# Attention sums of each edge visit: added to the table in memory by GpSimd, in place of TensorE's carry products

## What is computed

```
h = relu(layernorm(x));  y = layernorm(h) * g + b;  q, k, v = split(y @ Wqkv + bqkv)   # 8 heads of 32
scores = sum_d q[src] * k[dst] * SCALE                 # one per edge and head
e      = exp(scores - max over the edges of dst)
agg    = segment_sum(v[src] * e / segment_sum(e, dst)[dst], dst)
x1     = h + agg
x      = x + x1 + feedforward(layernorm(x1))           # gelu(y @ W_in + b_in) @ W_out + b_out
# second layer: h1 = relu(layernorm(x)); messages h1 @ W[relation], summed by dst, gelu, layernorm, added to x
```

## Time and profile before

| | us |
|---|---|
| median of 3 runs | 1527.08 |
| lowest and highest | 1525.3, 1531.56 |
| the profiled execution's own time | 1523.96 |
| its span in the trace | 1522.1 |
| TensorE busy in the span | 1138.3 (75%) |
| VectorE busy | 898.6 (59%) |
| GpSimd busy | 918.3 (60%) |
| ScalarE busy | 448.1 (29%) |

### The profile page before, as it was taken

One profiled execution on the slowest core, in us unless ns is written; L12 is line 12 of the kernel. 1 busy time (PEld: TensorE's weight loads), 2 busy tenths in 40 slices (PEclk: granted clock), 3 DMA queues, 4 the chain that ended last, 5 costly groups with the idle time before them and its releaser, 6 DMA issues.

```text
span 1522.1 us, 18355 instructions
## 1 busy us (share of the span) xinstructions
PE 1138.3 (75%) x5319; PEld 846.0 (56%) x5319; DVE 898.6 (59%) x2826; ACT 448.1 (29%) x1150; POOL 918.3 (60%) x983
## 2 busy tenths in 40 slices
PE   5784879999999999999999993554645555554543
PEld 2442667777787777777777652333534334443432
DVE  5762678878887887887888630133425443442425
ACT  4652224454454444445445330000000000000000
POOL 3855666666666666666666004666666666766651
PEclk9997899999999999999999996767767876776766
DMA  7768776777877777777676212333433343343431
GB/s 243 215 188 264 214 223 210 248 238 231 272 228 239 250 237 237 229 245 220 228 252 223 78 58 72 105 110 113 123 114 112 113 116 115 115 121 108 119 95 56
DMA packets 142977, 265.55 MB, mean 174 GB/s; under 512 B 41594, under 2 KB 89828, under 8 KB 139930
## 3 DMA queue, kind: packets, MB, share of 16 engines
q0 software_dynamic: 52480, 160.68, 35.3%
q1 hardware_dynamic: 89434, 102.48, 20.7%
q10 hardware_dynamic: 960, 1.18, 0.2%
HBM read 199.25 MB, written 65.01 MB: 174 GB/s over the span
## 4 chain that ended last, share of the span: by engine, by line
DVE 31%; issue 20%; another core or an unknown queue 18%; PE 18%; ACT 5%; DMA 0%; DVEq 0%; POOL 0%; POOLq 0%; ACTq 0%
DVE arena L1807 5%; DVE arena L1812 5%; PE ps L1539 5%; DVE arena L1742 4%; PE ps L1506 3%; PE ps L1679 3%; DVE arena L1860 2%; PE ps L1565 2%; PE ps L1495 2%; DVE arena L689 2%; ACT arena L1314 1%; ACT L1298 1%; DVE arena L692 1%; DVE arena L671 1%
## 5 line engine op out<-in xcount | busy, mean ns | idle before, releaser
L1222 POOL DMA_INDIRECT arena<-qv_tab,srcs x392 | 383.3, 978 | 229.4 <-PE ps L1506 127.4
L1265 POOL DMA_INDIRECT arena<-h_all,typs x392 | 376.1, 959 | 236.2 <-issue 112.9
L1679 PE MATMUL ps<-arena 128*128 128x256 f32 x784 | 248.1, 477 | 92.2 <-DMA arena<-h_all,typs 47.5
L1679 PEld LDWEIGHTS ps<-arena 128*128 128x128 f32 x784 | 184.5, 243 | 150.5 <-issue 52.1
L1506 PE MATMUL ps<-arena 128*128 128x264 f32 x784 | 213.7, 401 | 35.3 <-DVE arena L1742 24.4
L1565 PE MATMUL ps<-wrel,arena 128*128 128x512 f32 x400 | 188.0, 595 | 2.3 <-ACT arena L1330 2.3
L1506 PEld LDWEIGHTS ps<-arena 128*128 128x128 f32 x784 | 139.3, 193 | 73.8 <-DVE arena L1742 32.0
L1742 DVE TENSOR_TENSOR arena<-arena 128x512 f32<-128x512 f32 x196 | 143.8, 734 | 40.7 <-ACT arena L1298 33.4
L1495 PE MATMUL ps<-arena 128*128 128x264 bf16 x1032 | 143.4, 280 | 12.4 <-DMA arena<-k_tab 12.2
L1495 PEld LDWEIGHTS ps<-arena 128*128 128x128 bf16 x1032 | 125.6, 145 | 46.6 <-issue 37.2
L1807 DVE TENSOR_TENSOR arena<-arena,ps 128x512 f32<-128x512 f32 x172 | 117.4, 683 | 49.1 <-remote 24.0
(11 more groups left out here) (166 smaller groups left out, 1488.1 us busy)
## 6 DMA issues: line engine op xcount, KB each, us to landing
h_all<-arena SPq DMA_DIRECT2D x23, 1024.0 KB
arena<-dst SPq DMA_DIRECT2D x49, 256.0 KB
rel<-arena SPq DMA_DIRECT2D x77, 128.0 KB
arena<-k_tab SPq DMA_DIRECT2D x49, 198.0 KB
att<-arena SPq DMA_DIRECT2D x52, 132.0 KB, 5.4
qv_tab<-arena SPq DMA_DIRECT2D x25, 256.0 KB, 3.0
arena<-qv_tab,srcs POOLq DMA_INDIRECT x392
arena<-h_all,typs POOLq DMA_INDIRECT x392
```

Of the source, the lines that this page charges most:

```text
L1222: pool.indirect_dma_start(out=rowbuf[:, u * T + t, 0:2 * D], out_offset=None, in_=qv_tab, in_offset=bass.IndirectOffsetOnAxis(ap=srcs[:, v ...
L1265: pool.indirect_dma_start(out=rows1[:, u * T + t, :], out_offset=None, in_=h_all[0:N * R, :], in_offset=bass.IndirectOffsetOnAxis(ap=typs[ ...
L1679: last = nc.tensor.matmul(ps[:, 6 + u, 0:D], ind1[:, u, t, :], rows1[:, u * T + t, :], start=(t == 0), stop=(v == 0 and t == T - 1))
```

## The change

In the fused stage `carry`, its matrix `car`, the semaphores `car_ready` and `win_done` and SP's `store` go. TensorE's sum of a visit ends with its own last tile, and ScalarE's `take` waits for that. `osum` now holds the sums of that visit alone, and GpSimd adds them to the 128 rows of `att` by a DMA that reads the rows in memory and adds (`accum_op`). It is put between tiles 1 and 2 of GpSimd's gathers three visits later; the last three come after all gathers. Each waits until the one before has landed, as before.

```diff
-            car = cut([2, WIN])
@@ SP
-                def store(v):
-                    w = window(v)
-                    sp.wait_ge(osum_ready, v + 1)
-                    if v >= 1:
-                        sp.wait_ge(att_out, 16 * v)
-                    sp.dma_start(att[bass.ds(w, WIN), :], osum[:, v % 2, :]).then_inc(att_out, 16)
...
-                    if v >= 1:
-                        store(v - 1)
...
-                store(LASTV)
@@ GpSimd, in gather(v)
+                        if t == 1 and v >= 3:
+                            add_window(v - 3)
...
+                def add_window(v):
+                    w = pool.value_load(wof[0:1, v + 1:v + 2], min_val=0, max_val=NWIN * WIN)
+                    pool.wait_ge(osum_ready, v + 1)
+                    if v >= 1:
+                        pool.wait_ge(att_out, 16 * v)
+                    pool.dma_start(att[bass.ds(w, WIN), :], osum[:, v % 2, :], accum_op=ALU.add).then_inc(att_out, 16)
...
                 for v in range(G):
                     gather(v)
+                for v in range(G - 3, G):
+                    add_window(v)
@@ ScalarE, in take(v)
-                    act.wait_ge(win_done, v + 1)
+                    act.wait_ge(agg_done, PAIRS * (v + 1))
@@ TensorE
-                                                start=(t == 0), stop=(v == 0 and t == T - 1))
+                                                start=(t == 0), stop=(t == T - 1))
...
-                def carry(v):
-
-                    if v == 0:
-                        pe.wait_ge(agg_done, PAIRS)
-                        pe.sem_inc(win_done, 1)
-                        return
-                    pe.wait_ge(osum_ready, v)
-                    pe.wait_ge(car_ready, v)
-                    nc.tensor.matmul(ps[:, AGG, 0:AW], car[:, v % 2, :], osum[:, 1 - v % 2, :], start=False, stop=True).then_inc(win_done, 1)
...
-                        carry(v)
...
-                    carry(v)
@@ VectorE
-                        if j == 0 and v >= 1:
-                            nc.vector.tensor_scalar(car[:, u, :], iotaj[:, :], wcar[:, v:v + 1], None,
-                                                    ALU.is_equal).then_inc(car_ready, 1)
```

More of the change, by code:

```diff
@@ L721, in program @@
             row_in = [sem(f"rows_in{j}") for j in range(2 * PAIRS)]
-            indT_ready, car_ready = sem("indT_ready"), sem("car_ready")
+            indT_ready = sem("indT_ready")
             turn_ready, ind_ready = sem("turn_ready"), sem("ind_ready")
             exp_done, w_ready, agg_done = sem("exp_done"), sem("weighted_ready"), sem("summed")
-            win_done, osum_ready, att_out = sem("window_done"), sem("osum_ready"), sem("att_out")
+            osum_ready, att_out = sem("osum_ready"), sem("att_out")
             zeros = sem("zeros_ready")
```

## The result

| | before | changed |
|---|---|---|
| median, us | 1526.76 (4 runs) | 1557.6 (4 runs) |
| lowest and highest | 1525.3, 1531.56 | 1554.14, 1560.63 |
| ratio, 95% interval | | 1.0196, 1.0164 to 1.0227 |
| span of the profiled run | 1522.1 | 1552.4 |

The forecast, 1517.4 us with a range of 1508 to 1538, was wrong: the time lies above the range. The kernel before itself has two levels, 1525 to 1534 us in some sets of runs and 1433 to 1438 us in others (two sets, one at each level, ran on the chip of the same number), and the changed kernel is slower at the first level and faster at the second. I call them **the 1530 level** and **the 1436 level**; ratios are always between runs of one set.

What follows compares the result with a forecast made beforehand. Each pair of visits was taken as bound in turn by VectorE and TensorE. Terms -9.9 - 1.5 - 1.3 + 0 + 1.5 + 1.5 = -9.7 us took the median 1527.08 to 1517.4 us, range 1508 to 1538.

Steps and rivals of the forecast that it cites:

- Added: GpSimd's part: GpSimd, each visit: a register load and a DMA issue, 1.85 us, fit into some 2.1 us left idle; cost 0.
- (d): GpSimd becomes the bound if an adding store's issue takes 1 us more than a gather's: 37 us, 1554 us; chance 0.07.
- Removed: the carries: TensorE, fused stage: 48 carry products go, only 22 even visits' count, 0.45 us each: -9.9 us.
- the matrices: VectorE: 48 matrices for the carry go, one per pair counts, 22 x 0.07 us: -1.5 us.
- Moved: `residual`: GpSimd's addition comes 0.5 to 1.5 us later, off the `weigh` TensorE waits for; 0 to 0.12 us a pair, -1.3 us.
- the VectorE part: Stretch of each pair of visits, `statistics` to the end of `weigh`, where VectorE works without pause and TensorE waits.
- rival (b): Both carries of a pair count: 21.6 us in place of 9.9, 1505.7 us, pairs near 28.4 us; chance 0.08.
- Moved: the store, the weak point: GpSimd's later store before the block's load: 2.5 us to spare at one end, 0.35 late at the other; taken 0.
- Rival (a): The adding store lands late and `prepare` waits, 22 pairs times the wait; over 0.75 us, 1534 us and more: chance 0.11.
- Start, +1.5: First block's load lands at 200.9 to 203.8, 2.7 to 5.6 us late, partly hidden: between -1 and +4.5 us.
- End, +1.5: Last block, 23, comes 1.2 to 3.2 us later behind GpSimd's store; cost between 0.5 and 3 us.

Runs made afterwards that it cites:

- the first set: Changed kernel with carry gone and SP's plain store back, beside the kernel before: 1521.6 us, 0.9897, pairs of 28.95 us.
- the last: No carry and SP's plain store again, run at another time at the 1530 level: 1511.22 us, 0.9919 to the kernel before, pairs of 28.83 us.
- four runs without it: To the kernel before: store copying instead of adding 0.9921; GpSimd kept busy, SP's store, no carry 0.9941; adding store behind sixth gather 1.1126, at visit's end 0.9889.

## Why the prediction was wrong, step by step

- **The step that failed: "Added: GpSimd's part ... Cost 0, with little over."** I priced GpSimd by its own time and by the buffers it fills, and there the numbers are good: 1.04 us of issue and 0.30 of pause against 1.85 us expected, and GpSimd still waits for TensorE. But at this level GpSimd's store moves TensorE's signals: +3.1% and +1.9% of the kernel in the two pairs of runs that differ by it alone, about 2.4 and 1.4 us a pair. None of my rivals had it. (d) gave 1554 us, near the measured time, but it asked for GpSimd as a bound, which it is not: that its number fits is luck. Why the store moves the signals stays open.
- **Removed: the carries, -9.9 us, and the matrices, -1.5.** Right in size at the 1530 level: without carry and with nothing else changed the ratios 0.9897 and 0.9919 are 15.8 and 12.4 us. The pairs lose 0.40 us against 29.35 in the first set and 0.52 in the last.
- **Moved: `residual`, "between 0 and 0.12 us a pair": mis-sized.** At the 1436 level, where no signal hides it, the pair loses 1.14 us (29.54 to 28.40). From `statistics` to the end of the `weigh` that TensorE waits for, before and after:

```profile
533.22 0.42 DVE L1778 TENSOR_TENSOR xs<-xs,ps 128x256 f32<-128x256 f32 x1 [1.67 <-PE ps L1547]
...
548.81 1.22 DVE L1742 TENSOR_TENSOR arena<-arena 128x512 f32<-128x512 f32 x1
...
550.09 1.16 PE L1506 MATMUL ps<-arena 128*128 128x264 f32 x4 [0.72 <-DVE arena L1742]
```

```profile
531.55 0.42 DVE L1766 TENSOR_TENSOR xs<-xs,ps 128x256 f32<-128x256 f32 x1 [1.58 <-PE ps L1537]
...
546.81 0.73 DVE L1730 TENSOR_TENSOR arena<-arena 128x512 f32<-128x512 f32 x1
548.85 1.07 DVE L1730 TENSOR_TENSOR arena<-arena 128x512 f32<-128x512 f32 x1
...
547.59 1.16 PE L1506 MATMUL ps<-arena 128*128 128x264 f32 x4
```

  The stretch fell from 16.81 to 15.99 us; 0.49 of the 0.82 is the `weigh` itself, which no longer overlaps `residual` (now the next one does, at 548.85, as the step said). TensorE's wait of 0.72 is gone. So the VectorE part gave way by six times what I took for it (0.13), and the pair came out where rival (b) had put it, "near 28.4", though (b) had the second carry for a reason and more than half of the stretch's gain is the `weigh`. That one in eight `weigh`s overlaps `residual` is so in every pair: in the kernel before, 20 of 162 between 240 and 840 us do, 1.20 us in the mean against 0.68 for the others; in the changed kernel again 20, of 1.04. No run moves `residual` alone, so its share is read from the rows and not measured.
- **Moved: the store, the weak point, taken 0.** Right. It let SP go on 3.79 us after its issue, in the interval of 3.80 to 5.1 but for 0.01, and no steady block waited. (My sum had the load due at 497.05, where the earlier trace rows say 497.12, and its ends come out at 494.4 and 497.3 in place of 494.5 and 497.4; nothing hangs on it.) Rival (a) did not happen here; the run with the store four gathers later shows its price. The Trainium skill's doubled cost of the read side ("Collectives: The Full Stack", The bandwidth ceiling) did not show; the page speaks of rings that move large blocks, not of one small store. At the 1436 level SP could go on 3.66 us after the adding store's issue began and 3.31 after the copying one's (3.71 and 3.44 in the median of the blocks), and the difference is in GpSimd's issue:

```profile
501.37 1.04 POOL L1227 DMA_DIRECT2D att<-arena  x1
...
505.03 0.33 SPq L1126 DMA_DIRECT2D arena<-att  x1
```

```profile
502.93 0.59 POOL L1227 DMA_DIRECT2D att<-arena  x1
...
506.24 0.33 SPq L1126 DMA_DIRECT2D arena<-att  x1
```

- **Start, +1.5, between -1 and +4.5.** Right where it was read: the first block was taken at 202.18, inside the 200.9 to 203.8 forecast, and the stage starts 2.9 us later. At the 1436 level the kernel before reaches `prepare(0)` at 186.50, and the same late store costs 12.4 us there, half of what the pairs give. The kernels beside it say that it is the place of the store: with GpSimd busy and SP's own store the first `turn_y` comes at 192.26, with the copying store at 205.24. The wait of `prepare(0)` in the changed kernel:

```profile
197.70 0.32 DVE L1737 TENSOR_SCALAR arena<-arena 128x8 f32<-128x8 f32 x1 [9.31 <-DMA arena<-att]
```

- **End, +1.5.** The last wait grew from 7.35 us to 8.57, 1.2 us; right.

```profile
896.71 0.17 DVE L1737 TENSOR_SCALAR arena<-arena 128x8 f32<-128x8 f32 x1 [8.57 <-DMA arena<-att]
```

- **The sum at the 1436 level**, where the change does only what the forecast says: 24.3 us less between the first and the last `turn_y`, 12.4 more before, 0.3 less behind: 12.2 us of span (1436.8 to 1424.6); the ratio of the set is 0.9914. The forecast ratio was 0.9937, by a gain in the pairs of half the size and a cost at the start of an eighth.
- **What I could have seen, and what not.** I priced every engine as if a signal arrived when its work ends. The page of the kernel before has "another core or an unknown queue" with 18% of its chain, in a program that runs on one core, so somewhere that was not so. But the chain does not point at the pairs: of these 272 us 27 lie before 230 us and 245 in the third stage. And the kernel without carry has the same 18% and came out nearly as priced. The row nearer to the cause was the one of L1291 above: a late signal once a pair, which another order on GpSimd could move to a dearer place. What it would cost there no row of the kernel before could tell.

## The version to keep

The adding store at the end of the visit's own eight gathers beats both kernels at the 1436 level: 0.9889 and 0.9876 to the kernel before, and 1418.7 us against 1424.61 for the changed kernel beside it. It starts the fused stage earlier (the first `turn_y` at 200.78, in the changed kernel at 206.14) and its pairs are 0.1 us shorter. At the 1530 level it was not run, and no kernel here that computes all sums beats the kernel before: that one is to be kept there. The kernel with SP's store and no carry leaves out a part of the shared rows; it only says that no carry is worth 0.8 to 1.0% there, as long as GpSimd has no store in its sequence.

## What to carry to other kernels

Work put on an idle engine isn't free because that engine has time: see what else its issues do to the others, and measure it with the same work done into a place that nobody reads. Waits for "remote" in a program of one core say that here signals come later than the work that sends them: look in which stage they stand and who waits, and count on it that a change of order can move them to another engine, at a price that no recorded wait of the kernel before gives. And compare only within one set, with the kernel in question in every set: here four runs without it seemed to give a clean answer, and it was wrong.

## What the runs showed of the hardware

- Signals of TensorE arrived up to 3.44 us after the recorded (modelled) end of the products that carry them, three in a bunch 0.06 us apart, with the granted clock at 1.00.
- One kernel had two levels, 6% apart, on the chip of one number at different times. With the slower one go late signals, missing entries in the record of the semaphores (101 for 172 key signals) and a lower granted clock in the third stage (0.73 against 0.83 from 1000 to 1200 us).
- GpSimd took 1.03 us in the median to issue its adding store of 132 KB and 0.59 for the copying one; from the end of the issue to SP's next step it was 2.62 and 2.72 us in the rows shown.
- VectorE's `weigh` took 1.20 us in the mean where it overlapped an addition on GpSimd and 0.68 where it did not.
